# Two more states of a selective scan summed by rows on VectorE instead of through TensorE transposes, with the instruction orders of every engine laid out anew

## The reference: what is computed

```python
hidden, gate = split(einsum('blh,he->bel', xn, W_in))
hidden = silu(causal_conv4(hidden) + conv_bias)
dt, B, C = split(hidden.T @ W_x)             # 128, 16, 16
dts = softplus(dt @ W_dt + b_dt)
state_n[l] = exp(dts[l] * A_n) * state_n[l-1] + dts[l] * B_n[l] * hidden[l]     # 16 states n
y = (sum over n of C_n[l] * state_n[l] + hidden * D) * silu(gate)
out = x + y @ W_out + sum over experts e of w_e * ((silu(xn @ Wg_e) * (xn @ Wu_e)) @ Wd_e)
```

## Time and profile before

| what | value |
|---|---|
| median of 3 runs | 1346.49 us (1344.55 to 1347.49) |
| the profiled execution | 1342.44 us |
| its span | 1340.6 us |
| TensorE busy | 1301.6 us, 97% |
| TensorE weight loads busy | 1219.6 us, 91% |
| VectorE busy | 1239.6 us, 92% |
| GpSimd busy | 1233.9 us, 92% |
| ScalarE busy | 1213.2 us, 90% |

### The profile page before, as it was taken

The page is one execution under the profiler, slowest core; times in us unless marked ns, Lnnn a source line. Parts: engine busy times, 40 slices in busy tenths (PEclk is TensorE's granted clock), DMA queues, the critical chain, the costliest instruction groups (busy, mean ns, idle before and its releaser), DMA issues.

```text
span 1340.6 us, 26644 instructions
## 1 busy us (share of the span) xinstructions
PE 1301.6 (97%) x9222; PEld 1219.6 (91%) x9222; DVE 1239.6 (92%) x1644; ACT 1213.2 (90%) x2111; POOL 1233.9 (92%) x674
## 2 busy tenths in 40 slices
PE   6899999999999999999999999999999999999998
PEld 5889999999999999999999999999999899999987
DVE  3799999999999999999999999999999999999997
ACT  5879999999999999999999999999999899999984
POOL 2999999999999989999999999989999999999996
PEclk9999999999999999999999999999999999999999
DMA  7543443544444344443544444344443534434342
GB/s 193 160 144 118 143 120 115 152 115 132 139 127 135 112 136 127 139 120 118 149 120 126 136 128 138 114 132 131 139 122 116 148 114 134 139 113 142 109 146 80
DMA packets 189399, 174.95 MB, mean 130 GB/s; under 512 B 43185, under 2 KB 172241, under 8 KB 189265
## 3 DMA queue, kind: packets, MB, share of 16 engines
q1 hardware_dynamic: 150864, 121.86, 30.5%
q10 hardware_dynamic: 38400, 51.40, 13.6%
HBM read 167.92 MB, written 5.24 MB: 129 GB/s over the span
## 4 chain that ended last, share of the span: by engine, by line
POOL 27%; issue 21%; ACT 19%; DVE 18%; PE 12%; DMA 2%; ACTq 1%; SPq 0%; DVEq 0%; POOLq 0%
POOL state L571 14%; POOL moe L586 6%; ACT decay L657 5%; PE pair_ps L1003 5%; ACT L657 5%; ACT L665 4%; DVE state L878 4%; PE out_ps L1138 3%; POOL state L580 3%; DVE dt L865 3%; DVE u L891 2%; DVE decay L878 2%; DVE u L919 2%; ACT moe L665 2%; DVE moe L898 2%
## 5 line engine op out<-in xcount | busy, mean ns | idle before, releaser
L571 POOL TENSOR_TENSOR state<-du,b_rep 128x1024 f32<-128x1024 f32 x256 | 611.7, 2395 | 61.1 <-DVE u L891 59.3
L878 DVE TENSOR_TENSOR_SCAN state<-decay,state 128x512 f32<-128x512 f32 x448 | 534.2, 1212 | 21.1 <-ACT decay L657 16.4
L657 ACT ACTIVATE decay<-dt,neg_a 128x255 f32<-128x255 f32 x1024 | 436.7, 465 | 37.7 <-DVE state L878 19.0
L1138 PE MATMUL out_ps<-w_down,moe 128*128 128x256 f32 x1536 | 355.9, 381 | 3.1 <-POOL moe L586 1.9
L1138 PEld LDWEIGHTS out_ps<-w_down,moe 128*128 128x128 f32 x1536 | 282.5, 190 | 38.6 <-issue 4.1
L586 POOL TENSOR_TENSOR moe<-moe,rw_rep 128x512 f32<-128x512 f32 x192 | 249.3, 1309 | 8.7 <-DVE moe L898 7.3
L580 POOL TENSOR_TENSOR state<-state,c_rep 128x1024 f32<-128x1024 f32 x96 | 244.1, 2543 | 1.6 <-DVE state L878 1.6
L1003 PE MATMUL pair_ps<-xnT_hi,w_gate_hi 128*128 128x256 f32 x768 | 228.9, 298 | 3.2 <-DVE moe L898 3.2
L1003 PE MATMUL pair_ps<-xnT_hi,w_up_hi 128*128 128x256 f32 x768 | 225.7, 294 | 2.8 <-ACT moe L665 1.9
L657 ACT ACT_TABLE_LOAD x171 | 219.4, 1283 | 2.5
L1003 PE MATMUL pair_ps<-xnT_lo,w_gate_hi 128*128 128x256 f32 x768 | 216.4, 282 | 0.0
(11 more groups left out here) (149 smaller groups left out, 2252.5 us busy)
## 6 DMA issues: line engine op xcount, KB each, us to landing
w_down<-in_L_ffn_w_down_dram SPq DMA_DIRECT2D x384, 128.0 KB, 2.9
b_rep<-b_dram ACTq DMA_DIRECT2D x128, 256.0 KB, 3.3
rw_rep<-rw_dram SPq DMA_DIRECT2D x256, 96.0 KB, 2.7
c_rep<-b_dram ACTq DMA_DIRECT2D x128, 128.0 KB, 3.3
rw_rep<-rw_dram SPq DMA_DIRECT2D x256, 64.0 KB, 2.6
rw_rep<-rw_dram SPq DMA_DIRECT2D x256, 32.0 KB, 2.6
x_in<-L_attn_input_states_dram SPq DMA_DIRECT2D x16, 256.0 KB, 3.8
res<-L_attn_input_states_dram SPq DMA_DIRECT2D x16, 256.0 KB, 3.1
```

The source lines that it names most:

```text
L571: pool.tensor_tensor(state[:, n % STATES, :, :], du2[:, q, :, :], b_rep[:, n // BCH % 2, n % BCH, :][:, None, :].broadcast_to([P, ET, T]), ...
L657: last = act.activation(decay[:, h, j, 1:T], dt[:, q, e, 1:T], ACT.Exp, scale=neg_a[:, e, n:n + 1])
L878: dve.tensor_tensor_scan(a if n in ROWS_BY_VECTOR else x, a, x, 0.0, ALU.mult, ALU.add).then_inc(scanned, 1)
L1138: last = pe.matmul(out_ps[:, c, :], moe[:, p % RING, j, c * P:(c + 1) * P], w_down[:, p % RING, j, :], start=(p == 0 and j == 0 and c == 0 ...
```

## The change

States 11 and 13 move from `BY_TURN` to `ROWS_BY_VECTOR`: ten states are summed by row (four of them by VectorE alone) and six by turn. C_n is loaded for ten states a block instead of eight. No function changes. All lists of due times are replaced; those of blocks 1 to 14 (the middle list of each) and the whole of the short ones stand here, those of the first and last block are cut.

```diff
-    BY_ROW = [n for n in range(NS) if n in ((2, 4, 5, 6, 8, 9, 10, 12))]
+    BY_ROW = [n for n in range(NS) if n in ((2, 4, 5, 6, 8, 9, 10, 11, 12, 13))]
...
-    UNIT_AT[1]  [-3, -2, 4, 23, 26, 30, 30, 35, 36, 42, 45, 49, 49, 52, 55, 81, 85, 95, 101, 104, 108, 108, 114, 115]
+    UNIT_AT[1]  [-5, -4, 3, 13, 22, 23, 28, 28, 28, 31, 33, 45, 45, 49, 60, 66, 88, 90, 94, 94, 98, 107, 115, 118]
-    OUT_AT[1]   [32, 32, 41, 42, 69, 72, 89, 106, 110, 112, 137, 140]
+    OUT_AT[1]   [25, 25, 39, 44, 48, 77, 86, 98, 101, 114, 136, 140]
-    TURN_AT[1]  [[6, 6], [17, 19], [34, 34], [60, 69], [93, 94], [107, 108], [109, 109], [116, 116]]
+    TURN_AT[1]  [[5, 5], [13, 13], [24, 24], [53, 57], [109, 112], [119, 121]]
-    SILU_AT[1]  [-1, 12, 28, 39, 43, 55, 62, 71, 96, 97, 117, 120]
+    SILU_AT[1]  [2, 13, 35, 39, 43, 55, 69, 70, 97, 97, 117, 117]
-    SCALAR_ALONE[1]  {'conv_silu': -73, 'router_exp': -84, 'softplus': -20, 'first_state': 7, 'skip': 23, 'normed': -122, 'share': -62}
+    SCALAR_ALONE[1]  {'conv_silu': -60, 'router_exp': -80, 'softplus': -27, 'first_state': 7, 'skip': 24, 'normed': -124, 'share': -63}
-    GATE_SILU_AT[1]  [63, 68]
+    GATE_SILU_AT[1]  [54, 68]
-    MUL_AT[1]   [14, 23, 41, 46, 59, 63, 79, 92, 107, 108, 127, 129]
+    MUL_AT[1]   [12, 23, 44, 47, 54, 73, 79, 94, 105, 108, 127, 129]
-    ADD_AT[1]   [[20, 22], [64, 65], [84, 98], [104, 105], [114, 116], [120, 126], [130, 131]]
+    ADD_AT[1]   [[20, 22], [50, 55], [78, 110], [122, 126], [130, 130]]
-    ROW_ADD_AT[1]  [37, 49, [44, 47], 61, 78, [76, 76], 102, 119]
+    ROW_ADD_AT[1]  [38, 49, [43, 47], 62, 79, [74, 78], 98, [92, 94], 120, [107, 111]]
-    WEIGH_AT[1]    [17, 29, 37, 44, 65, 66, 80, 91, 99, 103, 131, 133]
+    WEIGH_AT[1]    [30, 30, 42, 44, 60, 67, 76, 95, 98, 110, 136, 136]
-    ROW_MUL_AT[1]  [21, 32, [43, 45], 55, 67, [72, 76], 90, 92]
+    ROW_MUL_AT[1]  [27, 42, [41, 45], 53, 66, [73, 78], 81, [90, 93], 97, [104, 108]]
-    C_LOAD_AT[1]   [-10, -10, 26, 40, 41, 61, 70, 80]
+    C_LOAD_AT[1]   [-1, 19, 28, 43, 43, 55, 70, 73, 91, 95]
...
-    ROWS_BY_VECTOR = [n for n in BY_ROW if n in ((5, 9))]
+    ROWS_BY_VECTOR = [n for n in BY_ROW if n in ((5, 9, 11, 13))]
...
-    WARM_AT = [[-119, 4], [-59, 15], [1, 50], [14, 7], [24, 6]]
+    WARM_AT = [[-63, 17], [-27, 34], [4, 17], [8, 5]]
```

More of the change, by code:

```diff
@@ L86, in build @@
[L86 to L110, removed]
@@ L130, in build @@
-    C_LOAD_AT = [[-11, 7, 26, 43, 44, 62, 69, 86], [-10, -10, 26, 40, 41, 61, 70, 80], [-22, -22, 31, 43, 57, 63, 82, 92]]
-    ROWS_BY_VECTOR = [n for n in BY_ROW if n in ((5, 9))]
+    UNIT_AT = [[-55, -32, -20, -13, 5, 5, 19, 26, 27, 32, 32, 41, 42, 48, 53, 59, 67, 81, 82, 90, 94, 100, 107, 110],
+               [-5, -4, 3, 13, 22, 23, 28, 28, 28, 31, 33, 45, 45, 49, 60, 66, 88, 90, 94, 94, 98, 107, 115, 118],
+               [-4, 5, 8, 15, 52, 59, 65, 65, 76, 96, 110, 114, 126, 136, 139, 144, 149, 149, 151, 159, 174, 195, 195, 204]]
@@ new lines, in build @@
+    OUT_AT = [[17, 24, 28, 39, 54, 78, 82, 83, 102, 106, 136, 140],
+              [25, 25, 39, 44, 48, 77, 86, 98, 101, 114, 136, 140],
+              [53, 73, 96, 122, 142, 143, 154, 154, 186, 213, 238, 251]]
+    TURN_AT = [[[4, 8], [9, 16], [17, 20], [45, 54], [109, 110], [117, 118]],
+               [[5, 5], [13, 13], [24, 24], [53, 57], [109, 112], [119, 121]],
+               [[9, 13], [30, 48], [60, 65], [113, 126], [188, 190], [205, 212]]]
+    TURN_Y_AT, PROJECT_AT = [[126, 131], [128, 129], [219, 234]], [148, 144, 253]
@@ new lines, in build @@
+    PE_FRONT = [{'xnT': -97, 'hid0': -91, 'hid1': -79, 'logits': -78, 'weightsT': -27, 'low': -63, 'lowT': -62, 'dt0': -55, 'dt1': -38},
+                {'xnT': -116, 'hid0': -113, 'hid1': -105, 'logits': -100, 'weightsT': -70, 'low': -67, 'lowT': -63, 'dt0': -52, 'dt1': -49},
+                {'xnT': -116, 'hid0': -115, 'hid1': -106, 'logits': -96, 'weightsT': -70, 'low': -66, 'lowT': -56, 'dt0': -54, 'dt1': -44}]
+    GATE_AT = [[36, 46], [38, 44], [60, 181]]
+    SILU_AT = [[-23, -10, 21, 32, 38, 55, 59, 69, 94, 94, 102, 120],
+               [2, 13, 35, 39, 43, 55, 69, 70, 97, 97, 117, 117],
+               [-1, 14, 37, 39, 50, 58, 71, 78, 84, 103, 184, 251]]
@@ new lines, in build @@
+    SCALAR_FRONT = [{'xnT': -92, 'hid0': -92, 'hid1': -90, 'weightsT': -13, 'low': -65, 'lowT': -61, 'dt0': -51, 'dt1': -44},
+                    {'xnT': -115, 'hid0': -107, 'hid1': -93, 'weightsT': -57, 'low': -52, 'lowT': -45, 'dt0': -41, 'dt1': -39},
+                    {'xnT': -114, 'hid0': -107, 'hid1': -93, 'weightsT': -57, 'low': -51, 'lowT': -47, 'dt0': -43, 'dt1': -37}]
+    SCALAR_ALONE = [{'conv_silu': -71, 'router_exp': -61, 'softplus': -35, 'first_state': 11, 'skip': 25, 'normed': -102, 'share': -23},
+                    {'conv_silu': -60, 'router_exp': -80, 'softplus': -27, 'first_state': 7, 'skip': 24, 'normed': -124, 'share': -63},
+                    {'conv_silu': -76, 'router_exp': -78, 'softplus': -28, 'first_state': 16, 'skip': 24, 'normed': -124, 'share': -60}]
@@ new lines, in build @@
+    GATE_SILU_AT = [[54, 68], [54, 68], [85, 212]]
+    MUL_AT = [[1, 7, 40, 46, 59, 63, 77, 89, 100, 106, 125, 129],
+              [12, 23, 44, 47, 54, 73, 79, 94, 105, 108, 127, 129],
+              [12, 25, 47, 50, 67, 70, 78, 88, 98, 119, 143, 181]]
+    ADD_AT = [[[24, 24], [57, 58], [104, 111], [125, 127], [131, 131]],
+              [[20, 22], [50, 55], [78, 110], [122, 126], [130, 130]],
+              [[38, 39], [49, 58], [86, 118], [140, 162], [209, 214]]]
+    ROW_ADD_AT = [[40, 53, [43, 46], 65, 78, [76, 77], 97, [90, 94], 123, [107, 110]], [38, 49, [43, 47], 62, 79, [74, 78], 98, [92, 94], 120, [107, 111]], [33, 48, [42, 47], 66, 87, [75, 76], 105, [89, 95], 215, [107, 108]]]
@@ new lines, in build @@
+    VECTOR_ALONE = [{'stats': -97, 'lo': -95, 'logits': -80, 'route': -31, 'taps0': -90, 'taps1': -83, 'total': 165},
+                    {'stats': -125, 'lo': -108, 'logits': -77, 'route': -67, 'taps0': -97, 'taps1': -86, 'total': 161},
+                    {'stats': -125, 'lo': -108, 'logits': -77, 'route': -67, 'taps0': -99, 'taps1': -88, 'total': 244}]
+    SUM_AT = [[133, 135], [134, 135], [229, 243]]
+    WEIGH_AT = [[18, 25, 31, 40, 58, 59, 84, 91, 100, 106, 130, 133],
+                [30, 30, 42, 44, 60, 67, 76, 95, 98, 110, 136, 136],
+                [14, 21, 45, 54, 62, 65, 85, 95, 101, 132, 177, 233]]
@@ new lines, in build @@
+    ROW_MUL_AT = [[24, 36, [43, 46], 47, 62, [72, 76], 87, [90, 93], 96, [105, 108]], [27, 42, [41, 45], 53, 66, [73, 78], 81, [90, 93], 97, [104, 108]], [18, 37, [42, 45], 54, 59, [74, 76], 73, [89, 95], 162, [107, 108]]]
+    POOL_ALONE = [{'rstd': -117, 'step_input': -16, 'gated': 152, 'select': -57},
+                  {'rstd': -128, 'step_input': -18, 'gated': 142, 'select': -71},
+                  {'rstd': -127, 'step_input': -23, 'gated': 253, 'select': -71}]
+    C_LOAD_AT = [[-21, 3, 34, 41, 49, 62, 73, 73, 90, 92], [-1, 19, 28, 43, 43, 55, 70, 73, 91, 95], [-21, -2, 26, 45, 51, 61, 73, 75, 92, 97]]
@@ L141, in pieces @@
+    SPLIT_VECTOR_AT = [-97, -75, -50, -46, -12, -9, 5, 6, 9]
+    SPLIT_SCALAR_AT = [-98, -88, -87, -74, -67, -67, -63, -54, -41, -40, -32, -23, -1, 0, 3, 3, 6, 8]
+    SPLIT_POOL_AT = [-100, -97, -95, -81, -32, -15, 13, 13, 13]
     def pieces(p):
```

24 lines of the change are left out of this document (removed).

## The result

| | before | after |
|---|---|---|
| median of 5 runs each | 1345.43 us (1341.42 to 1347.49) | 1351.64 us (1350.42 to 1352.19) |
| the profiled execution, its span | 1342.44, 1340.6 | 1352.19, 1350.4 |

The ratio is 1.0046, 95% interval 1.0029 to 1.0063: the changed kernel is slower by 6.2 us. The forecast was 1352, slower by 5.5. The runs of before lie in two groups, near 1342.5 us (granted clock mostly 0.998 and over) and near 1347 us (0.997 and under), so its median moves with the mix: 1345.4 in these five, 1343.6 in the 25 beside e5 to e8, against which the changed kernel is slower by 8.0. The number came out and its parts did not, so the text behind it is about where the 6 to 8 us are.

What follows compares the result with a forecast made beforehand. The prediction saw a balance of four engines 90% to 97% busy, with VectorE the hub the others wait for. +7.5 us for 14 blocks and -2 at the ends, from the 1346.5 us median, gave 1352 us, range 1330 to 1372.

Steps and rivals of the forecast that it cites:

- TensorE's turns, -1.7 us a block: TensorE, states 11 and 13: 16 transposes fewer give back 1.6 to 2.1 us a block, taken as 1.7.
- ScalarE, -1.9 us: ScalarE, middle block: four clears add 0.7 us, two table loads fewer save 2.6; net -1.9 us, as room only.
- VectorE, 78.8 us busy: VectorE, middle block: products and half sums replace turned sums, net +2.2 us, from 76.6 to 78.8 us busy.
- the one on the row sums: VectorE's row sums beside GpSimd's work: a new mix could move a block up to 1 us either way; taken as 0.
- Waits that come: VectorE's scans behind states 11 and 13: new waits for decays, 0.8 us a block at state 14, none at 12.
- The 0.2 at state 3: Stretch up to state 3: pair 0's silu now alone between state 1's decays, one more table pair, 0.2 us later.
- Idle time, 2.2 us: VectorE, middle block: 1.2 us of the old 3.9 us idle remains, plus new waits of 0.8 and 0.2 us.
- The sum, middle blocks: A middle block takes 81.0 us against 80.47, +0.5 us; +7.5 us for 14 blocks.
- The ends, -2 us: First and last block, not bound by VectorE: fewer turns and new lists give 0 to -4 us, taken as -2.
- the dense hub: Rival: VectorE, once the longest, is kept fed; a block takes 79.6 us, the kernel 1332 us; chance 0.32.
- The idle time that stays: Rival: VectorE already the bound, its 3.9 us idle a block stays; 82.7 us a block, 1376 us; chance 0.14.
- The untouched loop: Rival: GpSimd's three state inputs in a row and what precedes them keep the block; 1344 to 1349 us; chance 0.16.

Runs made afterwards that it cites:

- e5: Kernel before the change, turned sums of states 11 and 13 add only 64 of 512 columns (VectorE relieved): 1343.3 us, ratio 0.9999.
- e8: Changed kernel, turns of states 7 and 14 made twice, 16 transposes more a block (TensorE loaded): 1362.4 us, ratio to before 1.0146.
- e9: Kernel before the change, pair 3's silu made an exp, two table loads a block fewer (ScalarE relieved): 1344.2 us, ratio 1.0003.
- e10: Changed kernel, pair 3's silu made an exp, two table loads a block fewer (ScalarE relieved): 1352.0 us, ratio to before 1.0057.
- e6: Changed kernel, half sums of states 11 and 13 add only 64 of 512 columns (VectorE relieved): 1345.9 us, ratio to before 1.0018.
- e3: Kernel before the change, last block worked by the middle blocks' lists: 1351.7 us.
- e4: Changed kernel, last block worked by the middle blocks' lists: 1353.4 us.
- e11: Kernel before the change, weighing of pairs 1 and 8 on 64 of 512 columns (GpSimd relieved): 1338.7 us, ratio 0.9954.
- e1: Kernel before the change, states 11 and 13 moved to VectorE but in the old order: 1419.2 us, ratio 1.0547.

## Why the prediction was right in its number

- *TensorE's turns, -1.7 us a block:* right in its work (79.7 to 78.35 busy, 1.4), and right that VectorE's waiting for it would go (20.9 to 2.8 us in all).
- *ScalarE, -1.9 us:* right, 75.3 to 73.1. All table loads are 324 for 347: the decays' and the pairs' fell by 40 to 159 + 116, but those ahead of the gates' silu (L726) rose from 14 to 29. That it is only room is what e9 and e10 found at one place each.
- *VectorE, 78.8 us busy:* 78.0 (the sum unrounded gives 78.7). The added work came as priced, at 692 and 682 ns for each product and half sum. The step that failed is the one on the row sums, where I took 0 of a bound of 1 us: in the windows of the middle blocks they fell from 1545 to 1451 ns, (120.5 - 113.2) / 13 = 0.56 us a block. That is most of the 0.8; the rest may be fewer waits, since each adds an instruction's tail to the busy time, and was not taken apart.
- *Waits that come:* 0.8 at state 14, measured 0.67 in the block shown and 0.67 or 0.68 in four others. Right by its own working. The 0.2 at state 3 did not come: the scan there waits 0.24 us in middle blocks before and after.
- *Idle time, 2.2 us:* (1046.8 - 1013.95) / 13 = 2.5. The waits for the decays, 32.9 us over the kernel before, are 30.0, of which some 11 (16 x 0.67) are the new one at state 14: the old ones fell by 0.9 us a block, not 1.4.
- *The sum, middle blocks:* 81.0 forecast, 80.52 measured; +7.5 us became +0.7 over 13 blocks. This and the next are the terms that failed.
- *The ends, -2 us:* about +5.7, all in the last block. I had argued from busy shares before the change (TensorE 80.5 of 86.8 us) that VectorE does not bind there; after it e6 gets its whole relief back, and in the stretch through which the chain runs on VectorE it is busy 97.6%. The share over the whole last block (79.2 of 92.5) hides this. Of the 5.7 us some 3 are the lists (e3, e4). The start gives no clear difference: block 2's first scan stands at 207.7 before and 211.1 after, but at 207.9 to 212.9 over five profiled kernels with before's start and at 209.0 to 211.2 over six with the new one.

So the two profiled executions differ by 3.4 at the start, 0.7 in the middle and 5.7 at the end, 9.8 us in all, and the medians by 6.2, since before's profiled execution lies 3 us below its median. The forecast's 5.5 is +7.5 - 2. It was right by a sum of two errors of opposite sign, and by its base: counted from the profiled execution it said 1348, and that kernel's profiled execution took 1352.2. That is luck.

Of the rivals, the dense hub (1332 us) needed less than 1.6 us of idle time on VectorE and has 2.5. The idle time that stays (1376 us) falls with the measured idle time, 2.5 and not 3.9 us, and with e5: VectorE relieved before the change gave nothing. By the Trainium skill, "Perfetto Trace Analysis", "Identifying the Most-Contended Engine", VectorE with 95.2% against the weight loads' 93% would have been the engine to relieve first; the only relief that helped before is GpSimd's (94.0%), the second by that rule. The untouched loop, three state inputs in a row on GpSimd, stood in the chain that ended last with 14% of the span before (all state inputs) and has 1% after, so it is not what holds the block after. As a bound it is not refuted: e6 and e11 lie below 80.4 us, but both also shortened the row sums for which these inputs wait. Why both orders come to 80.5 us within 0.06 stays open: no run here tells a coincidence of two layouts from a common cause.

## What to carry to other kernels

Where four engines were over 90% busy, time taken off one was worth between nothing and a fifth of itself, and 16 transposes added cost 0.76 us: a move of work can't be priced on one engine alone. The order weighs as much, and a change of the work is to be compared only with an order laid out for it (e1: the same states, 4.3 us a block worse). Work the first and the last stage out for themselves, and look at stretches of them: VectorE was idle a seventh of the last block, and full in the half of it that counted. And a total that comes true proves no term of its sum; read each term off the profile after.

## What the runs showed of the hardware

Relief on VectorE came back as longer row sums: with two inputs in SBUF these take 1197 ns at best and up to 2276. In before's middle blocks the row sums that have a GpSimd tensor instruction beside them for under 30% of their time take 1.22 us on average and the others 1.88; in e5 it is 1.22 and 2.20. GpSimd's step input takes 3285 ns on average before and 2374 after, when it no longer meets one. e5 took 30 us off other VectorE instructions and the row sums grew by 14.6 us, because they met GpSimd's instructions at another point. The products and half sums in PSUM, of one input in SBUF at most, stayed at 692 and 682 ns with GpSimd 93% busy beside them. The Trainium skill has the rule, in "SBUF — State Buffer", "Who interferes with whom": an instruction of VectorE with two SBUF inputs and one of GpSimd that reads SBUF exclude each other, and who comes first blocks the other; the trace agrees (a sum that starts 1.79 us before the end of GpSimd's instruction takes 2.87 us, one that starts 0.88 before it 1.96). What it means here: a row sum in PSUM's banks buys freedom from GpSimd and pays with the wait for the bank.
